# A third bank for the score maxima, turns in the keys' bank, softmax sums in two chains, and a new order of issue

## The reference, cut to what matters

```python
# x (16, 128, 512), ctx (16, 2048, 512), all float32
x = x + cross_attention(layernorm(x), ctx)      # 16 query heads of 32, ONE key head and ONE value head
    Q = layernorm(x) @ Wq + bq                   # (16, 128, 16 heads, 32)
    K = ctx @ Wk + bk;  V = ctx @ Wv + bv        # (16, 2048, 32)
    out = softmax(Q K^T / sqrt(32)) V @ Wo + bo
x = x + delta_rule_memory(layernorm(x), Ww, Wr, decay, log_alpha)   # 4 heads of 128, chunks of 64,
                                                                    # inverse of a unit triangular matrix
x = x + moe(layernorm(x), Wg, w1, w2)            # 16 experts, top 1, 128 rows of capacity each, relu
```

## Time and profile before

| | us |
|---|---|
| median of 3 runs | 2082.02 (2079.54 to 2087.32) |
| the profiled execution's own time | 2085.92 |
| its span in the profile | 2084.1 |
| until the first score tile of batch 0 | 47.0 |
| batch 0, from its first score tile to that of batch 1 | 101.3 |
| batch 1 | 98.6 |
| batches 2 to 14, 13 of them | 1247.7, or 96.0 each |
| batch 15, to its sums | 101.1 |
| from there to the experts | 62.6 |
| experts | 425.8 |

### The profile page before, as it was taken

The page is one execution under the profiler, slowest core; times in us unless marked ns, Lnnn a source line. Parts: engine busy times, 40 slices in busy tenths (PEclk is TensorE's granted clock), DMA queues, the critical chain, the costliest instruction groups (busy, mean ns, idle before and its releaser), DMA issues. The chain is left out here.

```text
span 2084.1 us, 33310 instructions
## 1 busy us (share of the span) xinstructions
PE 2006.0 (96%) x11884; PEld 1316.3 (63%) x11884; DVE 1274.3 (61%) x2218; ACT 1101.0 (53%) x2029; POOL 1642.0 (79%) x1387
## 2 busy tenths in 40 slices
PE   7779999999999999999999999999999899999998
PEld 4335565656565555556555656555555889999998
DVE  5656777776776777776777777777762333333333
ACT  2555565656566656656565656665553143333333
POOL 1778999999999999998999999999896055555555
PEclk7789999999999999999999999999998999999999
DMA  6752131212121221312121212221200199999994
GB/s 225 212 133 62 57 106 46 77 47 76 59 65 66 67 69 54 100 37 95 44 77 44 77 66 57 68 64 24 96 1 17 66 377 354 352 352 355 357 357 172
DMA packets 105125, 262.16 MB, mean 126 GB/s; under 512 B 8576, under 2 KB 33920, under 8 KB 96256
## 3 DMA queue, kind: packets, MB, share of 16 engines
q1 hardware_dynamic: 96912, 234.92, 32.8%
q10 hardware_dynamic: 4464, 14.62, 2.4%
q0 software_dynamic: 3584, 10.49, 1.3%
HBM read 223.67 MB, written 25.72 MB: 120 GB/s over the span
## 5 line engine op out<-in xcount | busy, mean ns | idle before, releaser
L1041 POOL TENSOR_TENSOR psum<-psum,weights 128x512 f32<-128x512 f32 x896 | 1155.6, 1290 | 113.4 <-ACT weights L665 6.6
L835 DVE TENSOR_REDUCE mpart<-bank 128x1 f32<-128x512 f32 x1024 | 677.0, 685 | 353.9 <-PE bank L420 349.2
L665 ACT ACTIVATE weights<-bank 128x512 f32<-128x512 f32 x1024 | 589.1, 596 | 379.9 <-PE bank L433 363.6
L433 PE MATMUL bank<-qT,kT 97*128 97x512 f32 x1024 | 498.5, 494 | 20.9 <-DMA qT<-mrow 13.5
L420 PE MATMUL bank<-kT,qT 96*128 96x512 f32 x1024 | 431.4, 440 | 9.9 <-DVE mpart L835 5.2
L433 PEld LDWEIGHTS bank<-qT,kT 97*128 97x128 f32 x1024 | 193.8, 192 | 192.9 <-issue 102.6
L420 PEld LDWEIGHTS bank<-kT,qT 96*128 96x128 f32 x1024 | 198.4, 194 | 144.2 <-DVE mpart L835 73.1
L445 PE MATMUL bank<-weights,v 128*32 128x512 f32 x2048 | 267.5, 618 | 0.0
L1293 POOL TENSOR_TENSOR w2l<-w,w2h 128x1024 fp32r<-128x1024 f32 x64 | 202.0, 3157 | 78.0 <-PE ebank L1206 57.0
L1236 ACT ACTIVATE hh<-ebank 128x512 fp32r<-128x512 f32 x64 | 38.3, 598 | 226.6 <-PE ebank L1190 226.6
L1230 ACT CAST w2h<-w 128x2048 fp32r<-128x2048 f32 x64 | 121.5, 1898 | 43.1 <-DMA w<-in_w 43.1
(11 more groups left out here) (168 smaller groups left out, 2803.4 us busy)
## 6 DMA issues: line engine op xcount, KB each, us to landing
w<-in_w SPq DMA_DIRECT2D x48, 2048.0 KB, 20.1
w_first<-in_ctx SPq DMA_DIRECT2D x64, 1024.0 KB, 5.0
w_first<-in_w SPq DMA_DIRECT2D x16, 2048.0 KB, 12.0
dispatched<-route ACTq DMA_DIRECT2D x17, 513.0 KB, 8.9
dis<-dispatched SPq DMA_DIRECT2D x16, 513.0 KB, 3.5
qT<-qh SPq DMA_DIRECT2D x128, 64.0 KB, 2.1
qT<-qs SPq DMA_DIRECT2D x64, 64.0 KB, 2.1
xr<-in_x SPq DMA_DIRECT2D x16, 256.0 KB, 2.7
```

The costliest lines, as they stand in the source:

```text
L433: e.matmul(B_BANK[u % 2][:], kT[b % 2][0:3 * HD + 1, k * P:(k + 1) * P], qT[b % 2][0:3 * HD + 1, g * 512:(g + 1) * 512], start=True, stop= ...
L665: e.activation(p[n % NP], B_BANK[u % 2][:], ACT.Exp).then_inc(p_act.sem, 1)
L835: e.tensor_reduce(mpart[g % 2][:, 4 * (n % 4) + n // 4:4 * (n % 4) + n // 4 + 1], max_bank(b, g, n)[:], AX.X, ALU.max).then_inc(max_dve.se ...
L1041: e.tensor_tensor(acc[:], first, p[(UNITS * b + u) % NP], ALU.add).then_inc(psum_pool.sem, 1)
```

## The change

It does these things:

1. **Two chains of sums.** POOL adds units 2, 4, ... of a group into `psum` and units 3, 5, ... into a second accumulator `podd`, and at unit 15 adds the two. The number of adds stays 15 a group.
2. **A third bank for the maxima.** `A_BANK` has three banks, used in turn (`max_bank`, `max_read`). The third is what `T_BANK` was. For batch 15's tail it takes the parts that `T_BANK` had.
3. **Turns in the keys' bank.** The transposes of x and of the values go to `KV_BANK`, in one order with keys, queries and sums (`kv_uses`, `kv_read`).
4. **Keys in tiles of 32.** L501's 4 matmuls of 64 columns become 8 of 32, at rows 0, 32, 64 and 96. The sums are the same.
5. **No `kvlow` buffer.** ACT copies the half straight into `kvs`, and DVE adds into it in place.
6. **Start.** wq is the second load on SP, ahead of context chunks 1 to 3; ACT loads bias, x, wkv, then chunk 0. Of batch 0's query sends four go from ACT's queue, and two of its key chunks stand ahead of the queries.
7. **Zeros spread.** One write each 12 ticks (to tick 98 of step 1), and the wait for them moves from the start of step 1 to the first use.
8. **All tables of ticks are new**, so the order within each engine changes.

```diff
-STEADY = Prep(norm=-59, norm_pool=-59, xn=-29, xnt=15, xnt_act=21, qproj=[24, 26, 28, 31], q_dve=30, q_act=55,
-              q_pool=55, qsend=58, kv=[18, 42, 55, 70], kvlow=[18, 42, 55, 74], kvs=[20, 52, 67, 75], kh=[22, 54,
-              69, 81], kl=[23, 59, 71, 112], vt=[63, 90], vt_act=[61, 94])
+STEADY = Prep(norm=-32, norm_pool=-32, xn=-22, xnt=-15, xnt_act=-11, qproj=[28, 30, 31, 34], q_dve=30, q_act=36,
+              q_pool=33, qsend=52, kv=[23, 38, 50, 63], kvlow=[23, 37, 52, 63], kvs=[19, 38, 52, 67], kh=[31, 53,
+              68, 76], kl=[34, 57, 67, 78], vt=[45, 79], vt_act=[46, 79])
+FIRST = Prep(norm=4, norm_pool=4, xn=6, xnt=8, xnt_act=11, qproj=[11, 12, 13, 14], q_dve=15, q_act=16, q_pool=18,
+             qsend=19, kv=[5, 7, 23, 36], kvlow=[7, 10, 24, 40], kvs=[8, 11, 17, 74], kh=[9, 14, 34, 41], kl=[11,
+             14, 20, 101], vt=[20, 105], vt_act=[20, 62])
+LOAD_AFTER, W1_AT, ZERO_AT, ZERO_STEP = 4, 80, 34, 12
-PE_AT = dict(sums=11, x1=[18, 19, 20, 22], xn2T=34, V=[37, 38, 39, 40], rkT=42, I=46, X1=50, Vn=100, oT2=103,
+PE_AT = dict(sums=15, x1=[23, 25, 26, 28], xn2T=36, V=[38, 39, 40, 41], rkT=44, I=48, X1=52, Vn=100, oT2=102,
...
-MAX_AT = [-37, -35, -34, -33, -32, -30, -28, -27, -24, -23, -20, -19, -16, -14, -12, -10]
-MAX_TURN, MAX_ROW, PV_AT = -6, -8, [17, 17, 33, 37]
+MAX_AT = [-39, -38, -37, -35, -34, -31, -29, -29, -28, -25, -22, -21, -20, -16, -15, -13]
+MAX_TURN, MAX_ROW, PV_AT = -8, -9, [21, 22, 38, 38]
...
-        A_BANK, B_BANK, PV_BANK, T_BANK, KV_BANK, P_BANK = bank[0:2], bank[2:4], bank[4], bank[5], bank[6], bank[7]
+        A_BANK, B_BANK, PV_BANK, KV_BANK, P_BANK = [bank[0], bank[1], bank[5]], bank[2:4], bank[4], bank[6], bank[7]
...
             + [(TICKS * (b - 1) + prep(b).qproj[0], b, ("q", 0)) for b in range(B)]
+            + [(TICKS * (b - 1) + prep(b).xnt, b, ("x", 0)) for b in range(B)]
+            + [(TICKS * (b - 1) + t, b, ("v", m)) for b in range(B) for m, t in enumerate(prep(b).vt)]
             + [(TICKS * (b + 1) + PE_AT["sums"], b, ("s", 0)) for b in range(B)])]
...
+            return A_BANK[(17 * (HG * b + g) + n) % 3]
+
+        def max_read(b, g, n):
+
+            before_g, before_n = divmod(17 * (HG * b + g) + n - 3, 17)
+            if before_g < 0:
+                return None
+            return max_dve.at(0, KB * before_g + before_n) if before_n < KB else mrow_act.at(0, before_g)
...
-            for c in range(4):
+            weight(e, wq[:], "Wq").then_inc(wq_in.sem, 16)
+            for c in (1, 2, 3):
                 load_ctx(0, c)
...
                     for j in range(DC):
-                        rows = slice(64 * (j % 2), 64 * (j % 2) + 2 * HD)
-                        ins = e.matmul(KV_BANK[rows, :], wkv[:, j, :], cxT[c][:, j, :], start=j < 2, stop=j >= 2)
+                        for n in (0, HD):
+                            row = 2 * HD * (j % 2) + n
+                            ins = e.matmul(KV_BANK[row:row + HD, :], wkv[:, j, n:n + HD], cxT[c][:, j, :],
+                                           start=j < 2, stop=j >= 2)
...
-                if t >= 34 and t % 4 == 2 and (t - 34) // 4 < ZEROES:
-                    n = (t - 34) // 4
+                if t >= ZERO_AT and (t - ZERO_AT) % ZERO_STEP == 0 and (t - ZERO_AT) // ZERO_STEP < ZEROES:
+                    n = (t - ZERO_AT) // ZERO_STEP
...
             def add_weights(b, u):
                 g, k = divmod(u, KB)
-                if k == 0:
+                if k < 2:
                     return
+                n = HG * b + g
+                acc = podd if k % 2 else psum[n % 5]
                 e.wait_ge(*p_act.at(b, u))
...
+                if k == 2:
+                    if n >= 5:
+                        e.wait_ge(*sums_pe.at((n - 5) // HG))
+                elif k == 3:
+                    if n:
+                        e.wait_ge(*psum_pool.at(0, 15 * n - 1))
                 else:
-                    e.wait_ge(*psum_pool.at(b, 15 * g + k - 2))
-                    first = acc[:]
+                    e.wait_ge(*psum_pool.at(b, 15 * g + k - 4))
+                first = acc[:] if k >= 4 else p[(UNITS * b + u - 2) % NP]
                 e.tensor_tensor(acc[:], first, p[(UNITS * b + u) % NP], ALU.add).then_inc(psum_pool.sem, 1)
+                if k == KB - 1:
+                    e.wait_ge(*psum_pool.at(b, 15 * g + 13))
+                    e.tensor_tensor(psum[n % 5][:], psum[n % 5][:], podd[:], ALU.add).then_inc(psum_pool.sem, 1)
```

More of the change, by code:

```diff
@@ L160, in attention @@
         cxT = [w1_first[:, c, :].rearrange("p (c t) -> p c t", c=DC) for c in range(4)]
-        kvlow, kvs = sb("kvlow", [P, 512]), [sb(f"kvs{i}", [P, 512]) for i in range(2)]
+        kvs = [sb(f"kvs{i}", [P, 512]) for i in range(2)]
         v1 = [sb(f"v1{i}", [P, KB, HD]) for i in range(2)]
@@ L283, in summed @@
             g, k = divmod(n, KB)
-            return 15 * g + max(k, 1) - 1
+            return 15 * g + (k - 2 if k >= 2 else k)
         def heads(ap, n=DH):
@@ L693, in prepare @@
                     e.copy(qh[:], qs[:]).then_inc(q_act.sem, 1)
+                    if b == 0:
+                        e.wait_ge(*q_act.at(0))
+                        for h in range(4):
+                            send_part(e, 0, 1, qh, h).then_inc(q_in.sem, 16)
                 if t in prep(b).kvlow:
@@ L696, in prepare @@
                     e.wait_ge(*kv_pe.at(b, c))
-                    if b or c:
-                        e.wait_ge(*(kvs_dve.at(b, c - 1) if c else kvs_dve.at(b - 1, 3)))
-                    e.copy(kvlow[half(c), :], KV_BANK[half(c + 1), :]).then_inc(kvlow_act.sem, 1)
+                    if b and c % 2 == 0:
+                        e.wait_ge(*vT_pe.at(b - 1, c // 2))
+                        e.wait_ge(*kl_dve.at(b - 1, c + 1))
+                    e.copy(kvs[c // 2][half(c), :], KV_BANK[half(c + 1), :]).then_inc(kvlow_act.sem, 1)
                 if t in prep(b).kh:
@@ L863, in prepare @@
                     e.wait_ge(*kvlow_act.at(b, c))
-                    if b and c % 2 == 0:
-                        e.wait_ge(*vT_pe.at(b - 1, c // 2))
-                        e.wait_ge(*kh_act.at(b - 1, 2 * c + 3))
-                        e.wait_ge(*kl_dve.at(b - 1, c + 1))
                     e.scalar_tensor_tensor(kvs[c // 2][half(c), :], KV_BANK[half(c), :], bkv[half(c), :],
-                                           kvlow[half(c), :], ALU.add, ALU.add).then_inc(kvs_dve.sem, 1)
+                                           kvs[c // 2][half(c), :], ALU.add, ALU.add).then_inc(kvs_dve.sem, 1)
                 if t in prep(b).kl:
```

110 lines of the change are left out of this document (46 added, 64 removed).

## The result

The changed kernel takes 2140.61 us (median of 4 runs, 2137.23 to 2149.73). The kernel before, run between them, takes 2080.78 (2078.36 to 2087.32). The ratio is 1.028, 95% interval 1.026 to 1.030. The profiled execution has a span of 2135.1 us against 2084.1.

The account below looks back on a forecast made before the run. POOL was taken to set the steady 96.0 us a batch, PE close behind. Gains of 48 (steady), 9, 5, 11 and 2.5 sum to 75.5 us, from profiled 2085.9 to 2010.4, said as 2008; range 1982 to 2050.

Parts of the forecast that it names:

- Rival 4: DVE's L874 beside POOL: at its longest, 1.77 us, four a batch add 2.8 us; within the range, no chance given.
- Steady period: Batches 2 to 14: 92.3 us each instead of 96.0, the middle between 89 and 95.5, gaining 48 us.
- Third bank: PE's weight loads for maxima waited 3.6 us a batch for DVE; the bank is worth between 0 and 3.6.
- Keys in tiles of 32: PE's key chunks: no gain in themselves; tiled runs fall from 17 to 15, 0.5 us less a batch.
- Turns in the keys' bank: Nine uses a batch hand one bank on; cost taken as 0, as other PE work covers them.
- Batch 0: Gain of 11 us (6 to 17), from the maxima's DMA no longer waiting behind zeros and from POOL.
- Batch 15: Last batch, POOL full: gain of 9 us (7 to 13) from two chains and a smaller backlog.
- Batch 1: As the steady batches and 1.3 us more: gain of 5 us (1 to 8).
- Start: Before batch 0: gain of 2.5 us (-1 to 5); four sends on ACT's queue save 2.5.
- The prediction's own last step: From profiled 2085.9 to 2010.4 us, with the median 3.9 lower, given as 2008.
- bound of 90.4 us: Steady batch length used for the range's fast end; with 14, 7, 10, 2.5 at the ends it gives 1980.

Follow-up runs that it names:

- run 13: Changed kernel with the keys' low part of chunk 1 at tick 55 of DVE's order, not 57; POOL untouched: 2044.92 us, ratio 0.981.
- run 9: Changed kernel, but at unit 12 of each group POOL's add also waits for the add just before it (one gap a group): 2064.06 us, ratio 0.988.
- run 4: Changed kernel with the loads of the start in the order of the kernel before: 2141.63 us, ratio 1.028.
- run 3: Kernel before with two chains of sums alone, without the kvlow buffer: 2166.97 us, ratio 1.040.
- run 14: Changed kernel with the keys' low part of chunk 1 at tick 60, behind the memory block's Y: 2113.21 us, ratio 1.012.
- run 2: Changed kernel, but adds of units 5, 8, 11 and 14 also wait for the add just before them (gaps put back): 2032.96 us, ratio 0.975.
- run 12: Changed kernel with such waits on the add just before at units 5 and 8 alone: 2026.56 us, ratio 0.970.
- run 5: Kernel before with two chains and waits on the add just before at units 5, 8, 11 and 14, without kvlow: 2053.98 us, ratio 0.984.
- run 7: Run 2 with the maxima in two banks, not three: 2276.70 us, ratio 1.092.
- run 8: Run 2 with keys and values in 4 matmuls of 64 columns a chunk, not 8 of 32: 2039.89 us, ratio 0.978.
- run 11: Run 10 with batch 0's preparation in the order of the kernel before: 2026.68 us, ratio 0.971.
- run 6: Run 2 with the zeros written each 4 ticks as before, not each 12: 2045.46 us, ratio 0.981.
- run 10: Run 2 with the loads of the start in the order of the kernel before: 2029.73 us, ratio 0.972.

## Why the prediction was wrong, point by point

**Which step failed.** Rival 4, "DVE starved by a POOL without gaps". The mechanism was named, and put down as "At its longest, 1.77, four a batch add 2.8 us to DVE [...] It delays keys, not the path; within my range". Both halves failed. The size: I took the longest of the earlier trace rows, seen beside a POOL that had a gap before almost every add, as an upper bound for a POOL that has none. But the change removes exactly these gaps. One operation is held 8.25 us. The place: I set the delay against DVE's free time of a batch, as if it were spread; the delay comes in one piece, and behind it in DVE's queue stands `Y` of the memory block, for which PE waits 6.9 us. Run 13 shows it with POOL untouched: the one operation moved, the hold is gone but for one batch, and so is the loss. That batch 13 of the changed kernel was spared, and had 92.5 us, says the same.

**When is it held?** I went through all 1088 of these operations in the 17 kernels (before, changed, 15 runs), and through each start of a POOL instruction that they overlap. A "gap" is 0.06 us or more between the end of one and the start of the next.

| operations of the keys' low part | |
|---|---|
| overlap no start of a POOL instruction | 134 |
| overlap one start (got in there), gap ahead of it | 330 |
| overlap one start (got in there), no gap | 554 |
| overlap more than one (held) | 70 |
| starts that the 70 were held over: without gap, with gap | 321, 0 |
| hold ended at a start with a gap, elsewhere | 69, 1 |

Shown: no operation was ever held over a gap, and a hold ends at the first gap (run 9 put one in its way and it ended there, 14 times). The one that ended elsewhere (run 13) ended while POOL stood still, waiting for ACT's exponential. All 70 end 0.54 to 0.55 us after the end of a POOL instruction that no other follows at once. Shown too: without a gap it can go either way, 554 to 70, and the place at which the operation starts matters (run 13). Not settled: the rule. Held ones started 0.31 to 0.35 us before POOL's next start (changed kernel, runs 4 and 9), 0.87 to 0.93 (runs 3 and 13), 1.02 to 1.05 (run 14); but others at 0.31 and at 0.86 to 0.98 got in, among them the one of batch 13 in the changed kernel. How long the add's input had been ready isn't the rule either: 5.7 us for the held ones in the changed kernel and 5.6 for the one of batch 13 that got in, 6.0 us for those of run 2 that got in, 4.0 to 4.2 for the held ones of run 14. So run 2's gain isn't proof that gaps are needed, only that no hold came up with them. If no hold outlasts a gap, as in all 70, then none can pass more than three adds there.

The Trainium skill, "SBUF — State Buffer", section "Who interferes with whom", says that a DVE instruction with two SBUF inputs contends with a GpSimd instruction that reads SBUF. The same page of the Trainium skill, section "SBUF: two separate sides", says that whichever of the two starts first has the ports for its whole instruction. By that rule a wait is one add at most, and 1.28 + 0.68 = 1.96 us would be the worst (an estimate from the rule and the two durations here). The 554 agree with it (at most 1.79 us), and so does who is held: in the changed kernel the 1024 maxima, which read a bank, never took over 0.69 us, the 64 `kvs` (L871, one input from a bank) never over 0.76, and L938, with one input from a bank, stays at its 0.69. The 70 don't: after a whole add the turn went to the next add, up to six times.

**Steady period, 92.3 said.** With nothing held it is 93.2 (run 2) or 92.8 (run 12), and run 5 has 94.3 in the old order. The terms behind it came out: POOL's gaps and the wait for the maxima are as said, PE's busy time in run 2 is 1200.3 of 1211.1 us. I am 0.5 us a batch off in run 12, 0.9 in run 2, and 8.7 with the hold.

**Third bank, "between 0 and 3.6".** Right for the order of before, and the wrong question: taken away from the new order it costs 16 us a batch (run 7). The edits were priced one by one, and two of them only stand together.

**Keys in tiles of 32, priced at 0**, with 0.5 for fewer tiled runs: 0.38 measured together (run 8). Right in sum; a border of two kinds of tiles costs 0.12 to 0.13, half of the 0.24 that I took, and the chunk itself is 0.02 to 0.04 shorter.

**Turns in the keys' bank, 0.** Right in the steady stage (no wait of L501 for DVE or ACT is listed there in the changed kernel or in run 2), wrong at the start (run 11).

**Batch 0, 11 said, 6 to 17.** 16.7 measured. 9.2 of them are the spread zeros (run 6), as the mechanism said.

**Batch 15, 9 said.** 8.6 measured. **Batch 1, 5 said.** It lost 2.1, by a held operation; 94.1 in run 2 is a gain of 4.5.

**Start, 2.5 won, -1 to 5.** It lost 11.0. I counted the bias, the sends and two chunks of PE's work, and didn't follow chunk 0 of the context, which moved from the second load on SP to the fourth on ACT: 4.0 to 5.0 us (runs 4, 10). The rest is some 6 to 8 us. The four sends on ACT's queue, which I had as a gain of 2.5, are part of it: the send that the maxima waited for is no longer in their way, but the copies behind the sends on ACT are late (by 1.6 us in run 11, and by an estimated 2.1 in the changed kernel, where the copy of values starts 3.26 us behind its transposes and in run 11 1.16). The others are the shared bank and the half clock (see run 11); that split is read from timelines and not tested.

Without the hold the sum misses by 23 us of span (2031.9 in run 2 against 2084.1 - 75.5 = 2008.6): 14.7 at the start, 11.4 in the steady stage, 3.5 in batch 15 and 0.5 in batch 1, less 4.7 in batch 0 and 2.2 after the batches. (The prediction's own last step is loose too: 2010.4 less 3.9 is 2006.5, not 2008, and its bound of 90.4 us has no working. Neither matters beside the hold.) The hold costs 103 us of span (2135.1 against 2031.9).

## What to carry to other kernels

When a change takes the gaps out of one engine, ask what used those gaps, and don't bound its wait by rows that were taken with the gaps in place. Follow what stands behind a delayed instruction in its own queue, since a share of busy time says nothing of a delay that comes in one piece. And look at the longest of a group, not at its mean: 13 instructions of 34242 cost 5%, and two waits a group, or one instruction moved by two ticks, gave it back.

## What the runs showed of the hardware beyond that

- A DVE operation of 0.68 us that reads two SBUF operands was held for up to 8.27 us in the changed kernel, over six POOL adds in a row with 1.22 us from start to start, and ended 0.40 to 0.47 us after the start of the first POOL instruction that had a gap of 0.08 to 0.14 us ahead of it (changed kernel, runs 3, 4, 9 and 14).
- The POOL instruction at which it gets in is stretched, from 1.28 us to 1.53 or 1.59 with a gap ahead (run 9, changed kernel) and to 1.72 without (run 12).
- After 8.6 us in which PE was busy 1.71, its clock stood at 0.50 for 3.4 us of solid work (changed kernel).
- Issuing four query sends kept ACT from its next copy for 2.75 us (changed kernel).
- An add that waits for the one before it follows by 1.42 us, one that doesn't by 1.22 to 1.24 (runs 2, 9 and 12).

Not tried: the keys' low part on another engine, or with one input in a bank, which would say whether the two SBUF inputs are the cause. That they are is argued here from who is held, and not shown.
